# One reduction sums q's four terms, and the outputs go in three chunks instead of two

## The reference, cut to what matters

```python
def _derivative(q, p, drive, coupling, bias):
    i_couple = jnp.tanh(q) @ coupling.T
    dq = q - q ** 3 / 3.0 - p + drive + i_couple + bias
    dp = EPSILON * (q + ALPHA - BETA * p)
    return (dq, dp)
# one step: dq1..dq4 from q, q + DT/2 dq1, q + DT/2 dq2, q + DT dq3 (p alike)
q_next = q + DT / 6.0 * (dq1 + 2 * dq2 + 2 * dq3 + dq4)
p_next = p + DT / 6.0 * (dp1 + 2 * dp2 + 2 * dp3 + dp4)
q_next = jnp.clip(q_next, -CLAMP, CLAMP)
```

## Time and profile before

| | |
|---|---|
| time, median of 3 runs | 6047.53 us (6045.94 to 6048.6) |
| the profiled execution's own time | 6057.33 us |
| its span, first to last instruction | 6055.5 us |
| DVE busy | 5678.5 us, 94% |
| PE busy | 4516.8 us, 75% |
| ACT busy | 2596.6 us, 43% |
| mean granted clock of TensorE | 0.995 |

### The profile page before, as it was taken

The page is one execution under the profiler, slowest core; times in us unless marked ns, Lnnn a source line. Parts: engine busy times, 40 slices in busy tenths (PEclk is TensorE's granted clock), DMA queues, the critical chain, the costliest instruction groups (busy, mean ns, idle before and its releaser), DMA issues.

```text
span 6055.5 us, 592967 instructions
## 1 busy us (share of the span) xinstructions
PE 4516.8 (75%) x263627; PEld 3815.0 (63%) x263627; DVE 5678.5 (94%) x32584; ACT 2596.6 (43%) x12040; POOL 5.6 (0%) x16
## 2 busy tenths in 40 slices
PE   7887777777777777777777777777777777777777
PEld 3446666666666666666666666666666666666666
DVE  5569999999999999999999999999999999999999
ACT  3334444444444444444444444444444444444444
POOL 0000000000000000000000000000000000000000
PEclk8999999999999999999999999999999999999999
DMA  5100000000000000000000000000000000000000
GB/s 206 44 15 0 0 7 0 7 0 7 0 0 7 0 7 0 7 0 0 7 0 7 0 7 0 0 7 0 7 0 7 0 0 7 0 7 0 7 0 7
DMA packets 11597, 57.06 MB, mean 9 GB/s; under 512 B 2616, under 2 KB 2616, under 8 KB 8512
## 3 DMA queue, kind: packets, MB, share of 16 engines
q1 hardware_dynamic: 11056, 55.84, 2.3%
q10 hardware_dynamic: 528, 1.05, 0.0%
HBM read 40.11 MB, written 16.78 MB: 9 GB/s over the span
## 4 chain that ended last, share of the span: by engine, by line
DVE 81%; issue 8%; ACT 5%; PE 5%; DVEq 1%; DMA 0%; SPq 0%; ACTq 0%
DVE xb L646 44%; DVE turned_sums L796 14%; DVE tanh_parts L646 8%; ACT xb L422 5%; DVE xb L819 5%; DVE xb L855 2%; DVE xb L923 2%; PE ps L493 2%; DVE drive L934 1%; DVE xb L908 1%; DVE xb L884 1%; PE ps L511 1%; DVE xb L914 1%; PE ps L548 1%; PE ps L537 1%
## 5 line engine op out<-in xcount | busy, mean ns | idle before, releaser
L604 PE MATMUL ps<-coup,tanh_parts 128*16 128x96 f16 (+1 forms) x262272 | 4165.0, 219 | 1463.9 <-ACT tanh_parts L428 740.9
L604 PEld LDWEIGHTS ps<-coup,tanh_parts 128*16 128x16 f16 x262272 | 3652.9, 89 | 1976.6 <-ACT tanh_parts L428 924.5
L422 ACT ACTIVATE xb<-xb 128x24 f32<-128x24 f32 (+1 forms) x4098 | 940.4, 230 | 3091.9 <-DVE xb L646 3081.7
L646 DVE SCALAR_TENSOR_TENSOR xb<-xb 128x64 f32<-128x64 f32 x11267 | 2153.5, 214 | 70.0
L646 DVE SCALAR_TENSOR_TENSOR xb<-turned_sums,step_scale,xb 128x64 f32<-128x64 f32 (+2 forms) x6145 | 1561.2, 261 | 41.7 <-issue 0.4
L796 DVE STREAM_TRANSPOSE turned_sums<-ps 128x96 f32<-128x96 f32 (+1 forms) x4096 | 1281.5, 313 | 70.4 <-issue 69.1
L646 DVE SCALAR_TENSOR_TENSOR tanh_parts<-xb,tanh_parts 128x24 f16<-128x24 f32 (+1 forms) x4098 | 717.1, 175 | 15.6
L466 ACT ACTIVATE xb<-xb 128x64 f32<-128x64 f32 x2048 | 499.3, 244 | 0.0
L428 ACT ACTIVATE tanh_parts<-xb 128x24 f16<-128x24 f32 (+1 forms) x2050 | 471.1, 230 | 64.5
L819 DVE SCALAR_TENSOR_TENSOR xb<-xb 128x64 f32<-128x64 f32 x2049 | 450.8, 220 | 0.1
L440 ACT ACTIVATE tanh_parts<-xb 128x24 f16<-128x24 f32 (+1 forms) x2048 | 357.3, 221 | 32.2
(11 more groups left out here) (69 smaller groups left out, 914.7 us busy)
## 6 DMA issues: line engine op xcount, KB each, us to landing
xb<-in_x SPq DMA_DIRECT2D x8, 2048.0 KB, 7.9
drive<-in_x_pt SPq DMA_DIRECT2D x8, 2048.0 KB, 24.5
out_pt<-drive SPq DMA_DIRECT2D x16, 1024.0 KB, 4.5
drive<-in_coupling_t SPq DMA_DIRECT2D x8, 512.0 KB, 11.5
mask_v<-in_cond SPq DMA_DIRECT2D x8, 132.0 KB
probs<-in_wo ACTq DMA_DIRECT2D x1, 1024.0 KB, 5.6
w_qkv<-in_wq SPq DMA_DIRECT2D x1, 64.0 KB, 3.8
w_qkv<-in_wk SPq DMA_DIRECT2D x1, 64.0 KB, 5.2
```

The costliest lines, as they stand in the source:

```text
L422: nc.scalar.activation(cols(tanh_sb, CHUNKS[j]), cols(q, CHUNKS[j]), ACT.Tanh)\
L604: last = nc.tensor.matmul(product(s, j)[SQ * g:SQ * g + ROWS, :], tanh_parts[:, s % 2, k, :], coup[:, k, part, g, n0:n1, :].rearrange("p c ...
L646: return V.scalar_tensor_tensor(out=out, in0=a, scalar=factor, in1=c, op0=ALU.mult, op1=op1)
```

## The change

The outputs go in three chunks, of 2, 3 and 3 blocks, so a matmul has 64, 96 or 96 columns, and a stage has 192 matmuls in nine groups. The state (q, p and all sums of them) is kept in units of a power of two taken from the coupling, in which the product needs no scale. The four terms of the next q (`linear`, `curve`, the turned product of REST and the earlier one of FIRST) lie in one tile `terms`, 168 columns per block, at fixed distances: 24 or 40 columns and 80 columns. `q_of` is one TENSOR_REDUCE over these four (`summands`), with the batch row outside and the two distances inside. `with_first_part` and `base_of` are gone; `cubic_of` is `curve_of`, which multiplies by a `slope` that a new ACT instruction makes. Each stage has three `turn_product`, three `q_of` and three `rest_of`. `rest_of` of chunk 0 now stands behind the third `turn_product`. The units come in as per-partition factors: the clips take their limits from two columns of `limits`, and `less_q_of`, `look_ahead` and `trace` take a factor from a column in place of a constant or a plain addition.

```diff
-CHUNKS = [(0, 3), (3, 8)]
+CHUNKS = [(0, 2), (2, 5), (5, 8)]
 NCH = len(CHUNKS)
 
 
-ORDER = [(0, 0), (0, 1), (1, 0), (1, 1)]
+ORDER = [(0, 0), (0, 1), (0, 2), (1, 0), (1, 1), (2, 0), (1, 2), (2, 1), (2, 2)]
...
-TANH_SCALE = 4096.0
 COUP_EXP = 14
+
+
+TANH_EXP = 20
+STATE_EXP = COUP_EXP + TANH_EXP
+TANH_SCALE = [step * 2.0 ** TANH_EXP for step in STEP]
+
+
+
+
+TURNED = [0, 32]
+LINEAR = [88, 80]
+CURVE = [112, 120]
+SPREAD = [24, 40]
+PAIRS = 80
+TERMS = 168
...
-        def turned_sum(j, part):
-            return turned_sums[:, CHUNKS[j][0]:CHUNKS[j][1], B * part:B * (part + 1)]
-
-        def first_sums():
-            return turned_sums[:, :, B * FIRST:B * (FIRST + 1)]
+        def turned_product(s, j):
+            return terms[:, CHUNKS[j][0]:CHUNKS[j][1], TURNED[s % 2]:TURNED[s % 2] + SQ]
+
+        def linear(s):
+            return terms[:, :, LINEAR[s % 2]:LINEAR[s % 2] + B]
+
+        def curve(s):
+            return terms[:, :, CURVE[s % 2]:CURVE[s % 2] + B]
+
+        def summands(s, j):
+
+            lowest = 8 if s % 2 == 0 else 0
+            pairs = terms[:, CHUNKS[j][0]:CHUNKS[j][1], lowest:lowest + 2 * PAIRS].rearrange("p c (i x) -> p c i x", i=2)
+            pairs = pairs[:, :, :, 0:2 * SPREAD[s % 2]].rearrange("p c i (j y) -> p c i j y", j=2)
+            return pairs[:, :, :, :, 0:B].rearrange("p c i j b -> p c b i j")
...
             def tanh(q, j, count):
                 act.wait_ge(q_next[j], count)
-                nc.scalar.activation(cols(tanh_sb, CHUNKS[j]), cols(q, CHUNKS[j]), ACT.Tanh)\
-                  .then_inc(tanh_ready[j], 1)
-
-            def first_part_as_now(parity, j, count):
+                nc.scalar.activation(cols(tanh_sb, CHUNKS[j]), cols(q, CHUNKS[j]), ACT.Tanh,
+                                     scale=rho[:, 0:1]).then_inc(tanh_ready[j], 1)
...
+            def square_and_slope(stage):
+                nc.scalar.activation(square[:, :], q_st[stage][:, :], ACT.Square, scale=rho[:, 0:1])
+                nc.scalar.activation(slope[:, :], q_st[stage][:, :], ACT.Copy, scale=-STEP[stage] / 3)\
+                  .then_inc(square_ready, 1)
...
             def turn_product(s, j, now):
 
                 dve.wait_ge(product_done[j], now)
-                V.transpose(turned_sums[:, CHUNKS[j][0]:CHUNKS[j][1], :].rearrange("p c r -> p (c r)"),
-                            product(s, j)).then_inc(product_turned[j], 1)
+                V.transpose(turned_product(s, j), product(s, j).rearrange("p (c r) -> p c r", r=SQ))\
+                 .then_inc(product_turned[j], 1)
 
             def q_of(s, j, now):
 
                 if j == 0:
 
-                    dve.wait_ge(base_ready, now)
+                    dve.wait_ge(curve_ready, now)
                 dve.wait_ge(product_turned[j], now)
                 out = q_st[s + 1] if s + 1 < STAGES else q_raw
-                axpy(by_block(out, CHUNKS[j]), turned_sum(j, REST), step_scale[:, s:s + 1],
-                     by_block(base, CHUNKS[j])).then_inc(q_next[j], 1)
-
-            def rest_of(parity, j, made):
-
+                V.tensor_reduce(by_block(out, CHUNKS[j]), summands(s, j), AX.XY, ALU.add).then_inc(q_next[j], 1)
+
+            def rest_of(stage, j, made):
+
+                parity = stage % 2
                 dve.wait_ge(tanh_ready[j], made)
-                axpy(tanh_part(parity, j, REST), by_block(tanh_sb, CHUNKS[j]), TANH_SCALE,
+                axpy(tanh_part(parity, j, REST), by_block(tanh_sb, CHUNKS[j]), TANH_SCALE[stage],
                      tanh_part(1 - parity, j, FIRST), ALU.subtract).then_inc(rest_ready[j], 1)
...
-            def cubic_of(stage, made):
+            def curve_of(stage, made):
 
                 dve.wait_ge(square_ready, made)
-                V.scalar_tensor_tensor(out=cubic[:, :], in0=square[:, :], scalar=-3.0,
-                                       in1=q_st[stage][:, :], op0=ALU.add, op1=ALU.mult)\
-                 .then_inc(cubic_ready, 1)
-
-            def base_of(stage, made):
-
-                dve.wait_ge(cubic_ready, made)
-                axpy(base[:, :], cubic[:, :], -STEP[stage] / 3, z_first_part[:, :]).then_inc(base_ready, 1)
-
-            def with_first_part(stage, out, z_of_stage):
-
-                return axpy(all_blocks(out), first_sums(), step_scale[:, stage:stage + 1], all_blocks(z_of_stage))
+                V.scalar_tensor_tensor(out=curve(stage), in0=all_blocks(square), scalar=-3.0,
+                                       in1=all_blocks(slope), op0=ALU.add, op1=ALU.mult)\
+                 .then_inc(curve_ready, 1)
...
-                axpy(less_q[:, :], drive_step[:, :], DT, q_st[0][:, :], ALU.subtract)
+                axpy(less_q[:, :], drive_step[:, :], factors[:, 2:3], q_st[0][:, :], ALU.subtract)
...
-                V.tensor_scalar(p_st[:, :], p_raw[:, :], -CLAMP - SHIFT, CLAMP - SHIFT, ALU.max, ALU.min)\
+                V.tensor_scalar(p_st[:, :], p_raw[:, :], limits[:, 2:3], limits[:, 3:4], ALU.max, ALU.min)\
...
-                V.tensor_tensor(drive_b[:, :], drive_cols[:, bass.ds(at, COLS)], bias_b[:, :], ALU.add)
+                axpy(drive_b[:, :], drive_cols[:, bass.ds(at, COLS)], inv_rho[:, 0:1], bias_b[:, :])
...
-                V.tensor_scalar(q_st[0][:, :], q_raw[:, :], -CLAMP, CLAMP, ALU.max, ALU.min)\
+                V.tensor_scalar(q_st[0][:, :], q_raw[:, :], limits[:, 0:1], limits[:, 1:2], ALU.max, ALU.min)\
...
-                V.tensor_tensor(at, at, q_st[0][:, :], ALU.add).then_inc(traced, 1)
-
-
-            dve.wait_ge(setup, 8)
-            z_of_first().then_inc(setup, 1)
+                axpy(at, q_st[0][:, :], rho[:, 0:1], at).then_inc(traced, 1)
...
             def stage(s, now):
 
                 following = (s + 1) % STAGES
-                parity = following % 2
                 made = after(now)
                 turn_product(s, 0, now)
                 if s == 0:
                     y_of()
                 if s == 1:
-                    z_of_third()
+                    p_sum_g0()
                 if s == 2:
                     p_sum_r(2)
                 if s == 3:
-                    p_next()
+                    look_ahead((now + STAGES) * (COLS // STAGES))
                 q_of(s, 0, now)
+                turn_product(s, 1, now)
                 if s == 0:
                     z_of_second()
                 if s == 1:
-                    p_sum_g0()
+                    z_of_third()
                 if s == 2:
                     z_without_last(now)
                 if s == 3:
-                    look_ahead((now + STAGES) * (COLS // STAGES))
-                turn_product(s, 1, now)
-                rest_of(parity, 0, made)
+                    p_next()
                 q_of(s, 1, now)
+                turn_product(s, 2, now)
+                rest_of(following, 0, made)
+                q_of(s, 2, now)
+                rest_of(following, 1, made)
                 if s == 0:
                     y_less_g0()
                     q_sum_g0()
                 if s == 1:
                     q_sum_r1()
                     p_sum_r(1)
-                    drive_step_of((now + 2) * (COLS // STAGES))
                 if s == 2:
-                    with_first_part(3, z_rest, z_rest).then_inc(z_rest_ready, STAGES)
                     trace((now - 3) * (COLS // STAGES))
                 if s == 3:
                     clip_p()
                     clip_q(made)
+                rest_of(following, 2, made)
+                if s == 3:
                     drive_less_p(now)
-                rest_of(parity, 1, made)
                 if s == 0:
                     forecast_third(made)
-                    with_first_part(1, z_first_part, z2)
                     rise_of(1)
-                    cubic_of(1, made)
-                    base_of(1, made)
+                    curve_of(1, made)
                 if s == 1:
                     rise_of(2)
-                    with_first_part(2, z_first_part, z3)
-                    cubic_of(2, made)
-                    base_of(2, made)
+                    drive_step_of((now + 2) * (COLS // STAGES))
+                    curve_of(2, made)
+                    dve.wait_ge(curve_ready, made)
+                    q_sum_r2()
                     less_q_of()
-                    q_sum_r2()
                 if s == 2:
                     forecast_first(made)
-                    z_of_last(now)
+                    z_of_last()
                     p_sum_q3()
-                    cubic_of(3, made)
-                    base_of(3, made)
+                    curve_of(3, made)
                 if s == 3:
-                    z_of_first(now).then_inc(z_ready, STAGES)
+                    z_of_first(now)
                     g0_of()
-                    dve.wait_ge(z_ready, now)
-                    with_first_part(0, z_first_part, z)
-                    cubic_of(0, made)
-                    base_of(0, made)
+                    curve_of(0, made)
                 return made
```

(23 more changed lines are left out.)

80 lines of the change are left out of this document (37 added, 43 removed).

## The result

The changed kernel takes 6521.41 us (median of 4 runs, 6519.69 to 6523.93) against 6048.07 for the one before on the same chip (4 runs, 6045.94 to 6049.23). The ratio is 1.0783 (95%: 1.0765 to 1.0802): slower by 473 us.

The account below looks back on a forecast made before the run. It took DVE's list and the loop through ACT and PE as the bounds. Stages of 3.07 + 3.02 + 3.00 + 3.07 made 12.16 us a step against 10.975, +607 us over 512 steps: 6655 us, range 6390 to 6980.

Parts of the forecast that it names:

- The price of the reduction: `q_of` on DVE: 255 and 308 ns, or 0.18 and 0.23 us start to start, from L651's surcharge over contiguous reads.
- the contiguous price: A reduction over contiguous columns on DVE costs 1.04 ns a column: 0.22 us for 64 values, 0.25 for 96.
- Two bounds: DVE's own instruction list and the loop through ACT and PE, 2.63 us a stage before, lie close together.
- PE's part, 1.39: First matmul to next chunk 0 turn: 1.05 us of columns, 0.28 latency and restart, 0.06 for a second restart.
- the round of 3.00: Once from chunk 0's turn through ACT and PE to the next turn: 1.315 + 0.30 + 1.39 us, before 2.63.
- From turn to `rest_of`, 1.315: DVE's part of the loop, turn of chunk 0 to `rest_of` of chunk 0: 1.315 us, where it was 0.96.
- Stage 3, 3.07: Stage 3's time: DVE's list 3.05 us, round 3.06 with `look_ahead`'s column factor, two clips at 0.18; 3.07 in the sum.
- that idle time: Stages 0 and 2: DVE's list 0.4 us under the round, covering ACT's slope delay and most of the loop's bookkeeping.
- The cheap reduction: Rival: `q_of` reductions at the contiguous price, 0.13 and 0.16 us start to start; about 6370 us, or 6420; chance 0.17.
- The far-apart price: Rival: `q_of` reductions priced like the `axpy` with far-apart operands; about 12.75 us a step, 6960 us; chance 0.09.
- the group of 64 columns at 0.042: Rival: on PE a group of 64 columns costs what one of 96 does; +0.21 us a round, 7085 us; chance 0.08.
- The faster case: Rival: the loop through PE doesn't bind, DVE's list alone does; about 10.7 us a step, 5905 us; chance 0.05.

Follow-up runs that it names:

- run 4: Changed kernel with `q_of` as one axpy of two terms in place of the reduction, curve and FIRST product left out of q: 6032.55 us.
- run 6: Kernel before with the three chunks and the changed kernel's order of work, no reduction, no units: 6548.98 us against 6052.56 (1.0819).
- run 5: Changed kernel with the reduction summing four adjacent columns of the turned product, `linear` and `curve` left out of q: 6240.03 us.
- run 2: Changed kernel with constant scales in ACT's tanh and square, no slope instruction, linear term of q left out of the derivative: 6373.23 us.
- run 1: Changed kernel with `rest_of` of chunk 0 moved one place earlier, ahead of the third turn: 6708.54 us.

## Why the prediction was right, and where its sizes were off

**That it gets slower, and where.** Right. The new work on DVE (a turn, a `q_of`, a `rest_of` per stage, and reductions in place of updates) costs more than the two instructions that go. Run 4 takes the reductions away, run 6 adds the third chunk alone.

**The price of the reduction.** Right: 263 and 315 ns for 255 and 308. From start to start they take 0.17 and 0.23 (3007.14 to 3007.31, 3007.62 to 3007.85), for 0.18 and 0.23. L651, the nearest row by its distances, gave it; run 5 shows that both halves of the choice held, the contiguous price as well as the surcharge for distance.

**Two bounds.** Right, and shown by run 2: with ACT light, stage 2 is set by PE's round at 2.85 and stage 1 by DVE's list at 2.95. I had summed that list at 3.01. That stage 1 of the changed kernel then takes 3.06, near my 3.02, is luck: 0.10 of it is the wait for ACT. That DVE would be seen waiting for PE didn't come true in the changed kernel. The cause is the step that failed outright, below.

**The size: 473 and not 607.** The terms that were off, in us a step:
- *PE's part, 1.39, and so the round of 3.00.* Measured 1.31 to the turn (2.85 for the round), in run 2 too, where DVE waits for the product. A group of 64 columns takes what I had estimated. Matmuls of the changed kernel by form, running in 3008.79 to 3008.80 and to 3008.91:

```profile
L633 PE MATMUL ps<-coup,tanh_parts 128*16 128x64 f16 x4 | 0.2, 193 | 0.0
...
L633 PE MATMUL ps<-coup,tanh_parts 128*16 128x64 f16 x19 | 0.3, 193 | 0.0
```

  That is 15 in 0.11 us, a group of four every 0.029. So the columns (1.05) were right, and the 0.28 + 0.06 of latency and restart were too much; 0.26 is left. The second restart that I allowed for doesn't show: 16 groups at 0.029 and 32 at 0.042 are 1.81 us, and with the 0.2 of the last matmul that is the 2.01 which the 192 take. Nor does the first, before: 16 x 0.042 + 16 x 0.069 + 0.23 = 2.01, and the row has 2.02. Stage 2: -0.15.
- *From turn to `rest_of`, 1.315.* Measured 0.17 + 0.18 + 0.17 + 0.20 + 0.11 + 0.23 + 0.20 = 1.26. The first slot between turn and `q_of` is 0.18 for 0.20, and the update behind the second turn 0.11 for 0.135.
- *Stage 3, 3.07.* Measured 2.94. A factor from a column in the slot between a turn and the `q_of` that waits for it costs nothing, so `look_ahead` added nothing, against the 0.06 that I put there. The clips were dearer than my 0.18 (0.22 each from start to start), the step from `drive_less_p` to `z_of_first` cheaper.
- *Stage 0.* The total is 3.03 for 3.07, by two errors that cancel. The round is 0.15 shorter, and the bookkeeping of the loop sticks out (2.85 in one step, 3.21 in the next).

**ACT was not in the sum.** This is the step that failed: "that idle time covers what ACT's new `slope` instruction delays", and "most of the loop's bookkeeping" with it. I had only looked at the tanh of chunk 0 ("ACT is not in it"), not at what ACT does behind chunk 2. ACT has a slope more in each stage and a scale from a column in each tanh and square. A tanh of 24 columns takes 314 ns, with a constant 223, and a square 336 for 244 (run 2). Its chain behind the reduction of chunk 2 ends at the same time as PE's round, within about 0.01 us in stage 2 and in stage 0 without bookkeeping: from first matmul to turn it is 1.31 in both, as in run 2, where PE alone holds the turn. So there was no idle time left to cover anything. Run 2 gives the price: 148 us.

The sum of the four stages was predicted 12.16 and is 11.87. Stage 2 accounts for 0.15 of that through the round, stage 3 for 0.13.

**Where the number was lucky.** The sum had no term for ACT, and the kernel nearest to that sum is the one of run 2: 6373 us, 282 under the 6655 and just below the range of 6390 to 6980. The terms for PE's part and for DVE's lists were too high, the missing one for ACT gave back 148, and so 6521 lies in the range, at the low edge of the forecast's own 6520 to 6800.

**The rivals.** The cheap reduction falls by the 263 and 315 ns, though its total (6370 to 6420) lay as near as the forecast's. The far-apart price falls by the same rows, the group of 64 columns at 0.042 by the 0.029 above. The faster case falls by run 2, where DVE does wait for PE.

**What stays open.** How the 473 us split into independent causes isn't settled, and perhaps can't be, for the parts don't add: distances 281 (run 5), reduction against update 489 (run 4), ACT's columns 148 (run 2), third chunk +496 or -94 by what stands beside it. Each is the price with all else as it is. The new order of work was never run without the third chunk's instructions, nor the third chunk in another order, so the 496 are of both. Whether the 0.65 to 0.67 ns a value come from the lines of the memory or from the shape of the access pattern wasn't tried.

## What to carry to other kernels

Cost a change on every engine whose instructions it touches, at their durations and along the chain that they form; when two chains end within hundredths of a microsecond of each other, removing one gains nothing in that stage (stage 2 of run 2), and lengthening one costs at once (run 1). Fusing four terms into one reduction pays only if it is cheaper than the updates that it replaces: here 263 to 315 ns, twelve times a step and on the way to the tanh, for two updates a stage that lay off it. Look first for gaps between an instruction and its reader on the busiest engine: moving updates that were due anyway into them gave 1.9% with nothing added.
